# Slot rounds and pair blending of a hypergraph layer: row scaling shared with ScalarE, a tanh gate, scores as rows, projections moved back

## The reference

```python
h = x @ W
alpha = softmax(where(H.T > 0, leaky_relu(h @ a_node), NEG))      # nodes of each of 64 hyperedges
agg = einsum('ben,bnf->bef', alpha, h)
beta = sigmoid((h @ a_gn)[:, None, :] + (agg @ a_ge)[:, :, None])
all_he = elu(beta * h + (1 - beta) * agg)                         # a row for each edge and node
industry = (adj / deg) @ (x @ W_ind)
scores(f) = tanh(f @ fcW + fcb) @ av
coefs1 = softmax(where(H > 0, scores(elu(agg)), NEG))             # edges of each node
g = einsum('bne,benf->bnf', coefs1, all_he)
coefs2 = softmax([scores(industry), scores(g)])
out = coefs2[0] * industry + coefs2[1] * g
```

## Time and profile before

| what | value |
|---|---|
| median of 3 runs | 2270.8 us (2267.96 to 2271.24) |
| the profiled execution | 2270.87 us, its span 2269.2 us |
| busy: PE, DVE, ACT, POOL | 90%, 89%, 63%, 41% of the span |
| slot rounds, 130.4 to 315.3 us | 184.9 us; PE busy 159.8, DVE 148.3, ACT 54.7, POOL 166.6; clock 0.93 |
| end of the slot block, 315.3 to 326.5 us | 11.2 us; clock 0.79 |
| `blend_pairs`, 326.5 to 421.7 us | 95.2 us; PE busy 72.0, DVE 53.9, ACT 42.4; clock 0.61 |
| the three layers behind, 421.7 us on | 1847.5 us |

### The profile page before, as it was taken

One profiled execution on the slowest core, in us unless ns is written; L12 is line 12 of the kernel. 1 busy time (PEld: TensorE's weight loads), 2 busy tenths in 40 slices (PEclk: granted clock), 3 DMA queues, 4 the chain that ended last, 5 costly groups with the idle time before them and its releaser, 6 DMA issues. The chain is left out here.

```text
span 2269.2 us, 61376 instructions
## 1 busy us (share of the span) xinstructions
PE 2044.1 (90%) x26430; PEld 1350.7 (60%) x26430; DVE 2021.4 (89%) x2705; ACT 1420.8 (63%) x2236; POOL 926.4 (41%) x532
## 2 busy tenths in 40 slices
PE   5888878578788899999999999999999999998886
PEld 5655445345576566666666666666666666665554
DVE  7578876499666999999999999999999999999995
ACT  4422234489734676667766776666766667676774
POOL 2259960136400344444444444444544444432211
PEclk9999986588988999999999999999999999999998
DMA  3000000434311221211211211210210210124442
GB/s 128 1 1 0 0 0 1 91 61 68 47 25 47 49 39 39 53 35 39 44 35 40 53 33 32 53 44 30 46 42 30 58 39 21 35 58 66 72 67 48
DMA packets 176818, 94.73 MB, mean 42 GB/s; under 512 B 158552, under 2 KB 163864, under 8 KB 176432
## 3 DMA queue, kind: packets, MB, share of 16 engines
q1 hardware_dynamic: 176560, 90.94, 18.6%
HBM read 80.09 MB, written 10.83 MB: 40 GB/s over the span
## 5 line engine op out<-in xcount | busy, mean ns | idle before, releaser
L523 ACT ACTIVATE x_sb<-x_sb,hid_neg_max 128x1024 f32<-128x1024 f32 x576 | 661.7, 1154 | 287.1 <-DVE hid_neg_max L437 286.8
L446 DVE STREAM_TRANSPOSE hid_weights_t<-x_sb 128x1024 f32<-128x1024 f32 x576 | 711.9, 1236 | 1.6 <-ACT x_sb L523 1.2
L437 DVE CUSTOM_DVE_ANT_0 x_sb<-ps_score,adj_mask,row_scale 128x1024 f32<-128x1024 f32 x512 | 638.6, 1247 | 7.3 <-PE ps_score L312 6.1
L332 PE MATMUL ps_low<-hid_weights_t,hid_x_rep 32*64 32x256 f32 x18432 | 575.5, 383 | 10.0 <-ACT hid_share L553 9.6
L312 PE MATMUL ps_score<-hid_y_hi,hid_xs 128*128 128x512 f32 x1152 | 522.1, 453 | 33.4 <-DVE hid_neg_max L437 30.4
L332 PEld LDWEIGHTS ps_low<-hid_weights_t,hid_x_rep 32*64 32x64 f32 x18432 | 392.1, 132 | 167.7 <-issue 96.7
L312 PE MATMUL ps_score<-hid_y_lo,hid_xs 128*128 128x512 f32 x1152 | 456.3, 396 | 0.0
L629 POOL TENSOR_TENSOR hid_z<-hid_z,hid_inv_cols 128x1024 f32<-128x1024 f32 x64 | 194.6, 3041 | 552.3 <-ACT hid_z L531 552.3
L312 PEld LDWEIGHTS ps_score<-hid_y_hi,hid_xs 128*128 128x128 f32 x1152 | 217.0, 188 | 259.1 <-issue 153.3
L312 PEld LDWEIGHTS ps_score<-hid_y_lo,hid_xs 128*128 128x128 f32 x1152 | 218.5, 190 | 44.5 <-issue 15.0
L621 POOL TENSOR_TENSOR hid_y_wide<-hid_y_wide,hid_y_hi 128x1024 f32<-128x1024 f32 x63 | 151.2, 2400 | 185.1 <-ACT hid_y_wide L514 185.1
(11 more groups left out here) (367 smaller groups left out, 3054.9 us busy)
## 6 DMA issues: line engine op xcount, KB each, us to landing
hid_inv_cols<-hid_inv_rows SPq DMA_DIRECT2D x64, 512.0 KB, 3.8
hid_x_rep<-hid_row_space SPq DMA_DIRECT2D x64, 256.0 KB, 5.8
gat_x_rep<-gat_row_space SPq DMA_DIRECT2D x32, 256.0 KB, 5.4
gat_e_wide<-gat_e_space SPq DMA_DIRECT2D x8, 512.0 KB, 6.5
marks<-hid_mark_rows SPq DMA_DIRECT2D x8, 512.0 KB, 4.9
x_sb<-in_x SPq DMA_DIRECT2D x4, 512.0 KB, 5.7
hyp_neighbours<-in_adj SPq DMA_DIRECT2D x4, 512.0 KB, 6.9
edge_adj_high<-in_adj SPq DMA_DIRECT2D x4, 512.0 KB, 9.1
```

Source lines behind the costliest of these rows:

```text
L332: ins = pe.matmul(m.ps_low[c * F:(c + 1) * F, a, 0:NT * Q], x_rep[a * Q:(a + 1) * Q, batch_of(g) % 2, b, :], weights_t[a * Q:(a + 1) * Q, ...
L437: dve.tensor_tensor_reduce(ring[:, i % RING, :], m.ps_score[:, i % 2, :], mask, scale, HUGE, ALU.add, ALU.min, neg_max[:, g % 2, t:t + 1]) ...
L446: dve.transpose(weights_t[:, g % 2, :, t, :], ring[:, i % RING, :].rearrange("p (b j) -> p b j", j=Q)).then_inc(tile_turned, 1)
L523: act.activation(ring[:, i % RING, :], ring[:, i % RING, :], ACT.Exp, scale=-1.0, bias=neg_max[:, g % 2, t:t + 1], accum_out=row_sum[:, g ...
```

## The change

In the slot rounds:

- the gate is tanh(beta/2) instead of exp(-beta). The sigmoid is (1 + tanh)/2: DVE's `scale_away` adds the one in the same instruction that multiplies, and the half lies in a halved identity that `add_diff` multiplies with. L2268 and L2269 go.
- `rank` stays, and a counter `slot_no` (128 x 1) goes up; `pick` compares with it.
- the second step of `coef` stands behind the first two `scale_away`.
- tiles 2 and 5 are multiplied with `coef` by ACT, in two halves of four copies of 64 columns, behind exp 3 and 4, and 6 and 7. POOL adds in the order 0, 1, 3, 2, 4, 6, 5, 7.

After the rounds DVE doesn't scale `m.h` any more; `blend_pairs` scales all eight tiles. There, scores are computed as rows: `av`, repeated in 32 columns, is the weight, and 512 nodes stream, 4 calls for a pair. ACT takes exp of the 128 x 512 result, PE transposes it (`turn_scores`), and DVE reads every 32nd column. ACT's exp stands ahead of the root. `project(q)` stands behind `score(q + 2)` instead of behind `turn("z", q)`, and `take(q)` moves with it. DVE's `finish(q - 1)` stands behind `blend(q)`.

```diff
             def _(pe):
                 count = slot_count(pe)
+                pe.wait_ge(halved, 1)
...
-                        pe.matmul(row_banks(t)[0], m.ident[:], diff[:, t % 2, :], start=False,
+                        pe.matmul(row_banks(t)[0], half_ident[:], diff[:, t % 2, :], start=False,
...
-                    act.activation(beta[:], beta[:], ACT.Exp, scale=-1.0).then_inc(beta_exped, 1)
+                    act.activation(beta[:], beta[:], ACT.Tanh, scale=0.5).then_inc(beta_bent, 1)
...
+                    def scale_half(n, h):
+                        t = BY_ACT[n]
+                        act.wait_ge(share_ready, k * NT + t + 1)
+                        act.wait_ge(coef_taken, k + 2)
+                        for b in range(4 * h, 4 * h + 4):
+                            s = share[:, t % 4, b * F:(b + 1) * F]
+                            ins = act.activation(s, s, ACT.Copy, scale=pool_coef[:, t, b:b + 1])
+                        if h:
+                            ins.then_inc(act_scaled, 1)
...
+                        if t in (3, 4):
+                            scale_half(0, t - 3)
+                        if t in (6, 7):
+                            scale_half(1, t - 6)
...
-                    for t in range(NT):
-                        pool.wait_ge(share_ready, k * NT + t + 1)
+                    own = 0
+                    for t in ADD_ORDER:
                         s = share[:, t % 4, :]
-                        pool.tensor_tensor(by_batch(s), by_batch(s), along(pool_coef, t), ALU.mult)\
-                            .then_inc(scaled, 1)
-                        pool.wait_ge(scaled, k * NT + t + 1)
+                        if t in BY_ACT:
+                            pool.wait_ge(act_scaled, k * len(BY_ACT) + BY_ACT.index(t) + 1)
+                        else:
+                            own += 1
+                            pool.wait_ge(share_ready, k * NT + t + 1)
+                            pool.tensor_tensor(by_batch(s), by_batch(s), along(pool_coef, t), ALU.mult)\
+                                .then_inc(scaled, 1)
...
-                    link(dve.tensor_scalar(beta[:], beta[:], 1.0, None, ALU.add))
-                    link(dve.reciprocal(beta[:], beta[:]))
...
-                        dve.tensor_tensor(by_batch(diff[:, t % 2, :]), by_batch(row_banks(t)[1]),
-                                          along(beta, t), ALU.mult).then_inc(diff_ready, 1)
+                        dve.scalar_tensor_tensor(out=by_batch(diff[:, t % 2, :]), in0=along(beta, t), scalar=1.0,
+                                                 in1=by_batch(row_banks(t)[1]), op0=ALU.add,
+                                                 op1=ALU.mult).then_inc(diff_ready, 1)
...
-                    link(dve.tensor_scalar(rank[:], rank[:], -1.0, None, ALU.add))
+                    link(dve.tensor_scalar(slot_no[:], slot_no[:], 1.0, None, ALU.add))
...
-                            dve.tensor_scalar(pick[:], rank[:], 0.0, None, ALU.is_equal)\
+                            dve.tensor_scalar(pick[:], rank[:], slot_no[:, 0:1], None, ALU.is_equal)\
...
-                for t in range(SCALED):
-                    row = m.h[:, t, :, :]
-                    dve.tensor_tensor(row, row, along(coef_sum, t), ALU.mult)
...
-                    for t in range(NT):
-                        ins = pe.matmul(score_bank(q)[:, 2 * t + k:2 * t + k + 1], apart[:, k, t * P:(t + 1) * P],
-                                        av[:], start=True, stop=True)
+                    for c in range(2):
+                        row = (2 * k + c) * 32
+                        ins = pe.matmul(score_rows[row:row + 32, :], av[:].to_broadcast([P, 32]),
+                                        apart[:, k, half(c)], start=True, stop=True)
                     ins.then_inc(scored, 1)
+
+            def turn_scores(q):
+                pe.wait_ge(exped, q + 1)
+                if q:
+                    pe.wait_ge(score_taken, q)
+                for t in range(4):
+                    ins = pe.transpose(m.ps_low[:, 2, t * P:(t + 1) * P], score_exp[:, t * P:(t + 1) * P], m.ident[:])
+                ins.then_inc(score_turned, 1)
...
             for q in range(1, QB):
                 score(q)
+                if q >= 2:
+                    project(q - 2)
                 if q + 1 < QB:
                     turn("h", q + 1)
+                turn_scores(q)
+                if q + 1 < QB:
                     find_hidden("h", q + 1)
                 turn("z", q - 1)
-                project(q - 1)
+            project(QB - 2)
             turn("z", QB - 1)
             project(QB - 1)
...
             for q in range(1, QB):
+                exp_scores(q)
                 root(q - 1)
-                exp_scores(q)
+                if q >= 2:
+                    take(q - 2)
...
-                h = m.h[:, SCALED:NT, 2 * q:2 * q + 2, :]
-                dve.tensor_tensor(h, h, coef_inv[:, SCALED:NT, 2 * q:2 * q + 2].unsqueeze(3)
-                                  .to_broadcast([P, NT - SCALED, 2, F]), ALU.mult).then_inc(h_scaled, 1)
+                dve.tensor_tensor(pair(m.h, q), pair(m.h, q),
+                                  coef_inv[:, :, 2 * q:2 * q + 2].unsqueeze(3).to_broadcast([P, NT, 2, F]),
+                                  ALU.mult).then_inc(h_scaled, 1)
...
+                blend(q)
                 if q:
                     finish(q - 1)
-                blend(q)
                 centre(q)
```

More of the change, by code:

```diff
@@ L2093, in hypergraph_layer @@
             pool_coef = psb("pool_coef", [P, NT, B])
+            slot_no = psb("slot_no", [P, 1])
+            half_ident = psb("half_ident", [P, P])
             step, picked, small_ready, rows_ready, rows_taken = (
@@ L2109, in hypergraph_layer, with place @@
             block = part.enter_context(nc.Block())
+            BY_ACT = (2, 5)
+            ADD_ORDER = (0, 1, 3, 2, 4, 6, 5, 7)
+            def place(t):
+                return ADD_ORDER.index(t) + 1
             def along(v, t):
@@ L2249, in _ @@
                 dve.memset(coef_sum[:], 0.0).then_inc(step, 1)
-                dve.wait_ge(step, 2)
+                dve.memset(slot_no[:], 0.0).then_inc(step, 1)
+                dve.tensor_scalar(half_ident[:], m.ident[:], 0.5, None, ALU.mult).then_inc(halved, 1)
+                dve.wait_ge(step, 3)
                 dve.nop().then_inc(rows_taken, 3)
                 dve.nop().then_inc(coef_taken, 1)
-                steps = 6
+                steps = 4
                 dve.tensor_scalar(pick[:], rank[:], 0.0, None, ALU.is_equal).then_inc(picked, 1)
@@ L2258, in _ @@
                 with dve.Fori(0, count) as k:
-                    link = Chain(dve, step, 2 + k * steps)
+                    link = Chain(dve, step, 3 + k * steps)
                     dve.wait_ge(small_ready, k + 1)
@@ L2438, in _ @@
             turn("h", 1)
+            turn_scores(0)
+            find_hidden("h", 1)
             turn("n", 2)
[L2440 removed]
             turn("n", 3)
@@ L2475, in exp_scores @@
                 act.wait_ge(scored, 2 * q + 2)
-                act.activation(first[:, q, :, :], score_bank(q).rearrange("p (t k) -> p t k", k=2), ACT.Exp,
-                               scale=-1.0).then_inc(exped, 1)
+                if q:
+                    act.wait_ge(score_turned, q)
+                act.activation(score_exp[:], score_rows, ACT.Exp, scale=-1.0).then_inc(exped, 1)
             def square(q):
@@ L2514, in _ @@
                 square(q)
-                take(q - 1)
             root(QB - 1)
+            take(QB - 2)
             copy("z", QB - 1)
```

34 lines of the change are left out of this document (18 added, 16 removed).

## The result

The changed kernel takes **2251.9 us** (median of four runs, 2251.2 to 2255.0), the kernel before 2270.9: a ratio of **0.9924, 95% interval 0.9909 to 0.994**. That is 19.0 us less, where 11.3 were forecast. The profiled execution is the longest of the four (span 2253.3).

| stage | before | after | difference | forecast |
|---|---|---|---|---|
| start to the first gate sum | 132.8 | 133.7 | +0.9 | +0.25 |
| first gate sum to the end of the last share | 182.5 | 168.9 | -13.5 | -7.2 |
| from there to the first scaling of `blend_pairs` | 11.3 | 10.9 | -0.4 | +0.8 |
| first scaling to the end of the last projection | 93.7 | 79.8 | -14.0 | -5 |
| layers behind | 1849.0 | 1860.1 | **+11.1** | 0 |

The account below looks back on a forecast made before the run. VectorE's head of a slot round was taken as the bound, with GpSimd nearly full and TensorE's chain next. From 2270.87, -6.2 for the slot part and -5 for blend_pairs gave 2259.7, stated as 2259.5 us; range 2250 to 2268.

Parts of the forecast that it names:

- Head of a round, -0.9: Slot rounds: first share starts at 218.7 instead of 219.60, bound by TensorE's chain; 0.9 us a round, 7.2 us in all.
- rival B: Slot rounds: TensorE's clock no longer falls at the head; round 18.8 us, -14.4, total 2252.3; chance 0.12.
- The first round, nothing: First slot round: GpSimd is idle and the gate's addition took only 0.2 us, so it gains nothing.
- The removed instructions are worth nothing beyond 0.9: Head of a slot round: removed instructions add up to 3 us but gain only 0.9, since TensorE is next.
- GpSimd 1.2 us ahead, counter without a wait: Slot rounds: GpSimd ends 1.2 us before the next first share; VectorE's counter just misses its last sum, without a second wait.
- rival C: Slot rounds: VectorE's small instructions wait for GpSimd twice (0.95 and 1.05); gain 0.1 a round, total 2266; chance 0.13.
- Copies on ScalarE 1.04: Slot rounds: four copies of 64 columns at 0.26 each take 1.04 us, hidden in idle time before exponentials.
- rival D: Slot rounds: ScalarE's copies take 0.37 each, four 1.48; the 0.9 are eaten, total 2266.9 or 2269; chance 0.10.
- Compare, nothing: Slot rounds: the compare with slot_no keeps its 1024 columns and its length; zero, with +-0.3 a round for the range.
- Tail +0.8, L2311 nothing: After the last round: four more ScalarE copies add 0.8 us; removing L2311's 7.64 us, beside that chain, gives nothing.
- blend_pairs -5: blend_pairs: scaling +0.7, first distance -4, second -1.7, third 0, tail +2, high clock -2; bounds +4 to -12.
- F's condition: blend_pairs: row scores no faster than columns, 0.63 or more each, against 0.43 (3.78 / 8) seen; total 2276.4; chance 0.05.

Follow-up runs that it names:

- before_filled: Kernel before, plus four unread matmuls a slot round in TensorE's two pauses at the turn of a round; 2273.6 us, ratio to before 1.0001.
- slot_no_only: Kernel before with one edit: slot_no counts up and rank is compared with it, instead of rank counted down; 2262.8 us, ratio to before 0.9963.
- rank_counted: Changed kernel with the whole rank counted down again each round and slot_no standing still; 2265.7 us, ratio to before 0.9972.
- column_scores: Changed kernel with scores as 128 x 1 columns again, exponential over 16 columns, no turns, new order kept; 2257.2 us, ratio to before 0.9936.
- blend_filled: Changed kernel plus unread matmuls on TensorE ahead of its waits in blend_pairs, 2 to 12 at a place; 2241.4 us, ratio to before 0.9855.
- pool_alone: Changed kernel with all eight tiles scaled by GpSimd in order of tiles, no copies on ScalarE; 2255.3 us, ratio to before 0.9929.
- gate_by_exp: Changed kernel with the gate as exp, plus one, reciprocal and the whole identity again; 2252.4 us, ratio to before 0.9923.

## Why the prediction was right or wrong

- **What bounds before**: right as to VectorE's head. Rows 2 to 4 left open what TensorE's low clock cost there; before_filled shows: nothing.
- **Head of a round, -0.9**: the failed step. It held 0.63 for the first matmuls of the changed kernel too. Where a round did run low, the head was 6.36 us, as 7.25 - 0.9 says, and the round 19.7, as forecast. But only the first and one other did; the other heads were 5.25, rounds 18.6. In those TensorE is not the bound: the exponential ends at 194.81 and the share starts at 195.30, right behind L2322, which ends with GpSimd's addition. This is rival B, to which I gave 0.12. The argument against it, "the gap is there in any case", is refuted: the gap stays at 0.77, and it is 0.53 in slot_no_only as in rows 4, with the clock high in both. What keeps the clock up is not shown. TensorE's idle time behind its first additions goes some way: 1.59 us before and up to 1.88 in rank_counted, with a fall in every round behind the first, 1.16 in the changed kernel and 0.76 in slot_no_only, with few. But the one later round of the changed kernel that fell had 1.17 ahead of it, like its neighbours, so that is not all.
- **The first round, nothing**: it took 1.4 us more, since its head ran at the low clock; in column_scores and blend_filled, with the same rounds, it took the 18.6 of before.
- **"The removed instructions are worth nothing beyond 0.9"**: the credit was wrong as well. From 20.57 the counter alone leads to 19.8 (slot_no_only). With the counter and the later step of `coef`, the tanh leads to 19.4 (pool_alone), ScalarE's tiles to 18.8 (gate_by_exp), and both to 18.7 (means behind the first round). With `rank` back 1.8 us of it are lost. So the two edits that I had at nothing, the counter and ScalarE's tiles, carry the rounds, as far as the step of `coef` leaves that open. The tanh, beside the other edits, is worth 0.1.
- **GpSimd 1.2 us ahead, counter without a wait**: the counter took 0.14, and rival C is out. The margin is gone, since the round became shorter by as much. GpSimd's idle time is 0.70, not over 1.5. L2314 and L2322, each with two operands in SBUF, were held (0.99 and 0.59; at best 0.31 and 0.23, in a round of pool_alone), the counter with one was not. The Trainium skill, GPSIMD Engine Reference, its table of figures, names VectorE's instructions with two SBUF inputs, and the trace agrees. The gate's addition and `rank`, with one operand each, were held too. The same table names instructions in a two-port mode beside those with two inputs; no row says in which mode these ran.
- **Copies on ScalarE 1.04**: 1.05. The exponential of tile 7 comes right behind them, and its share 0.4 us later than before; rival D's 1.48 didn't occur. What they save on GpSimd is worth 0.7 us a round (pool_alone), where I had them only as a cost.
- **Compare, nothing**: 0.76 where it was 1.17, a little better than the +-0.3. The operand is not the reason: slot_no_only has it and takes 1.17, rank_counted has zero in its place and takes 0.75.
- **Tail +0.8, L2311 nothing**: -0.4; the copies cost about what was said (0.7), the product behind took 1.99 in place of 3.01 at the high clock. VectorE is idle 9.29 us ahead of the first scaling, so L2311 was hidden, as said.
- **blend_pairs -5**: the direction was right, the size wrong; -14 is beyond my bound of -12. By part: start +0.4 (+0.7 forecast), first distance -3.8 (-4), second -6.8 (-1.7), third -3.3 (0), tail -0.6 (+2), and the -2 for high levels had no place of its own. Two terms failed. The second distance was given a projection ahead of its transposes, but `project(q - 2)` starts only at pair 2, so there is none in it: with the 2.1 of a projection in it, 11.9 would be 14.0, as the third is 13.8. And the walk was taken halfway between the levels, at 17.0, when most steps of these distances met the high one, for which 14.3 had been worked out. The scores, taken at 1.9 to 2.0 at the high level, took 1.06 where both halves were ready. The Trainium skill, TensorE: Matmul & The Clock Gate, Part 3, has column tiles run beside each other; here eight instructions in 1.06 us are 1.9 times faster than my row-based value, and the trace agrees that they overlap.
- **F's condition**: 3.78 / 8 is 0.47, not 0.43. It changes nothing; the row scores were faster than either.
- **"The layers behind start as much earlier" and are unchanged**: wrong by 11 us in the profiled execution, and by 7 to 9 in the others if their changed stages took the same. I had no term and no rival for it.
- **The total** lies inside the range by luck. The changed code gained 28 us where 11 were forecast, and the layers behind, for which nothing was forecast, took 11 of them back. Had they kept their length, the total would have been near 2243, below my 2250. It came near rival B's 2252.3, but by another sum: -13.5 and -14 less what was given back, not -14.4 and -5.

## What to carry to other kernels

A low clock that is read in a trace belongs to the kernel around it: before keeping a matmul's slow duration for the changed kernel, ask which waits of TensorE change, and price both levels as two cases. Write out the new order of an engine pair by pair before adding up a distance; one pair may lack a step that the others have. Where TensorE waits in short pieces, unread matmuls in its pauses are cheap and here gave 8 us in one block; but they do nothing where another engine holds the path, and they can delay the first round. Unchanged code behind a change need not keep its length: here it took up to 11 us more in one execution, and six executions of one kernel lay 17 us apart. Give that a range of its own.

## What was not expected of the hardware

- The same unchanged layers took 1848.8 to 1860.1 us in single executions of kernels that differ only ahead of them. Runs of one kernel spread as far (before: 2264.8 to 2278.7 in one group), so how much of it goes with the kernel is open. In the stage that was looked into, there were three falls of the granted clock before and four after.
- Eight instructions of 512 columns on weights of 32 columns took 1.06 us, the eight of the fc_w product 1.99 at the same clock.
- An instruction of 1024 columns with one operand in SBUF took 0.69 us beside an idle GpSimd (rank_counted) and 1.64 beside its addition (before_filled).
